# Two-layer attention and FFN kernel on one core: which units stand in front of the scores, how the projection triples are dealt over the slots, and one visit for a head group's contexts

## The reference, cut to what matters

```python
xn = _layernorm(x)
s = L0_attn(xn)          # qkv = xn @ qkv_w + qkv_b; 32 heads of D = 16; rope on q and k
                         # scores = q k^T / 4 + causal mask; softmax; ctx = probs @ v; ctx @ out_w + out_b
g = silu( (silu(xn @ W_gate.T) * (xn @ W_up.T)) @ W_down.T )     # F = 1376, kept as 11 tiles of 128
x = x + s * g
xn = _layernorm(x)
s = L1_attn(xn)          # 4 layers of a recurrence with an MLP, as a scan over 512 positions
g = silu( octonion FFN of xn with ternary weights )
x = x + s * g
```

## Time and profile before

| | |
|---|---|
| three runs | 627.14, 627.68, 629.33 us; median 627.68 |
| the profiled execution | 627.55 us, of which the span is 625.6 us |
| PE busy | 603.1 us (96%), 3368 matmuls |
| POOL, DVE, ACT busy | 388.1, 380.0, 297.6 us |
| slots 0 to 10, first and second pass | 39.5 us and 37.5 us |

### The profile page before, as it was taken

How to read it: one execution, slowest core, us unless ns; L and a number is a source line. 1 busy time by engine, 2 the same in 40 slices (tenths; PEclk the granted TensorE clock), 3 DMA queues, 4 the chain that set the end, 5 groups by cost and what they waited for, 6 DMA issues and landing times.

```text
span 625.6 us, 9856 instructions
## 1 busy us (share of the span) xinstructions
PE 603.1 (96%) x3368; PEld 418.3 (67%) x3368; DVE 380.0 (61%) x908; ACT 297.6 (48%) x460; POOL 388.1 (62%) x598
## 2 busy tenths in 40 slices
PE   6997999999999999989999999999999999999996
PEld 5875655656657888656555666688887676767664
DVE  5955868666526489667686663265986261516257
ACT  3634767555643633356665557346122344232432
POOL 6776967555334578779576544346988495731364
PEclk9998999999999999999999999999999999999999
DMA  8797684744522327667768554835410000000002
GB/s 290 242 305 220 169 237 140 222 133 110 145 67 68 102 84 205 170 187 205 208 175 231 168 144 145 312 99 187 164 73 1 0 2 1 0 1 1 0 35 101
DMA packets 60369, 83.63 MB, mean 134 GB/s; under 512 B 17936, under 2 KB 26768, under 8 KB 60320
## 3 DMA queue, kind: packets, MB, share of 16 engines
q1 hardware_dynamic: 57968, 75.02, 40.6%
q10 hardware_dynamic: 2352, 8.00, 3.4%
HBM read 65.17 MB, written 26.99 MB: 147 GB/s over the span
## 4 chain that ended last, share of the span: by engine, by line
PE 78%; ACT 4%; DVE 4%; issue 3%; POOL 1%; DMA 1%; POOLq 0%; SPq 0%; ACTq 0%; DVEq 0%
PE proj_ps L967 8%; PE proj_ps L969 6%; PE proj_ps L968 6%; PE ctx_ps L1123 6%; PE score_ps L997 4%; PE proj_ps L1171 3%; PE proj_ps L1172 3%; PE scoreT_ps L1006 3%; PE score_ps L967 3%; PE score_ps L969 2%; PE score_ps L968 2%; PE scoreT_ps L967 2%; PE scoreT_ps L968 2%; PE scoreT_ps L969 2%; DVE score_ps L1518 2%
## 5 line engine op out<-in xcount | busy, mean ns | idle before, releaser
L784 POOL TENSOR_TENSOR w_lo<-raw,w_hi 128x512 fp32r<-128x512 f32 x98 | 130.9, 1340 | 76.0 <-ACT w_hi L1336 70.5
L1518 DVE CUSTOM_DVE_ANT_0 score_ps<-score_ps,causal 128x512 f32<-128x512 f32 (+3 forms) x256 | 118.6, 519 | 66.1 <-PE score_ps L997 65.3
L1379 ACT ACTIVATE probs_T<-scoreT_ps 128x1024 f32<-128x1024 f32 x80 | 82.1, 1027 | 67.6 <-PE scoreT_ps L1006 66.1
L967 PE MATMUL proj_ps<-xn_hi,w_hi 128*128 128x512 f32 x224 | 98.9, 441 | 7.5 <-DVE gate_silu L1569 5.2
L969 PE MATMUL proj_ps<-xn_lo,w_hi 128*128 128x512 f32 x224 | 88.9, 397 | 0.0
L968 PE MATMUL proj_ps<-xn_hi,w_lo 128*128 128x512 f32 x224 | 88.9, 397 | 0.0
L967 PEld LDWEIGHTS proj_ps<-xn_hi,w_hi 128*128 128x128 f32 x224 | 42.2, 188 | 35.5 <-issue 23.1
L815 POOL TENSOR_SCALAR_AFFINE_SELECT probs_T<-probs_T 128x256 f32<-128x256 f32 x128 | 54.3, 448 | 5.6 <-ACT probs_T L1379 5.6
L942 POOL TENSOR_TENSOR hsL<-hidden_T,hsH 128x256 fp32r<-128x256 f32 x44 | 38.1, 884 | 26.6 <-ACT hsH L1458 26.1
L782 POOL TENSOR_SCALAR w_hi<-raw 128x512 fp32r<-128x512 f32 x50 | 33.9, 679 | 25.8 <-PE proj_ps L969 25.0
L969 PEld LDWEIGHTS proj_ps<-xn_lo,w_hi 128*128 128x128 f32 x224 | 42.4, 189 | 10.1
(11 more groups left out here) (314 smaller groups left out, 1351.8 us busy)
## 6 DMA issues: line engine op xcount, KB each, us to landing
raw<-w SPq DMA_DIRECT2D x98, 256.0 KB, 2.9
rows<-rows_hi SPq DMA_DIRECT2D x32, 256.0 KB, 3.4
arranged<-tern SPq DMA_DIRECT2D x96, 85.0 KB
q_st<-rows SPq DMA_DIRECT2D x32, 200.0 KB
k_st<-rows SPq DMA_DIRECT2D x32, 200.0 KB
rows<-rows_lo SPq DMA_DIRECT2D x16, 256.0 KB, 4.0
gate_w<-arranged ACTq DMA_DIRECT2D x4, 704.0 KB, 6.5
up_w<-arranged ACTq DMA_DIRECT2D x4, 704.0 KB, 7.5
```

The source lines that it names most:

```text
L784: nc.gpsimd.tensor_tensor(w_lo[n % SPLIT][:, :], raw[n % RAW][:, :], F32(w_hi[n % SPLIT][:, :]), ALU.subtract).then_inc(unit_ready, 1)
L967: nc.tensor.matmul(acc, lh, rh, start=first, stop=False)
L1379: nc.scalar.activation(probs_T[g % 2][x][:, :, :], scoreT_ps[:, :, :], ACT.Exp, scale=0.25).then_inc(probs_ready, 1)
L1518: m = nc.vector.tensor_tensor_reduce(out=block, in0=block, in1=causal[:, S - w:], scale=1.0, scalar=-3e38, op0=ALU.add, op1=ALU.max, accum ...
```

## The change

Four things are altered. (1) `Q_UNIT` and `K_UNIT`: the second quarters of q and k become units 6 and 7, in front of slot 0; the first two pairs of the FFN become units 8 to 11. DVE then does both rotations in front of its row maxima of slot 0 (`units_after(0)`), and the FFN results of slot 0 behind them; `rope_slot`, `rounded_in` put the rounding, the rest and the writes one slot earlier for these two. (2) `pv_in`: all four key tiles of a group in one visit, in slot 11 + 5g. (3) ACT's copy of the sums moves to slot 12 + 5g and the turn to slot 14 + 5g. (4) `triple_slot` reads a table, made by `deal()`: it adds up what each slot holds besides triples, gives triples by the room that is left, at most 3 in a slot as a rule, and starts no unit u before the second slot after the one in which unit u - 2 ended. Slots 16, 21, 26, 31, 36 and 41 (context visits) get no triple, slot 44 gets 4.

```diff
-Q_UNIT, K_UNIT, V_UNIT = (0, 8, 12, 18), (1, 9, 13, 19), 2
-FFN_UNIT = [6, 7, 10, 11, 14, 15, 16, 17] + list(range(20, 34))
+Q_UNIT, K_UNIT, V_UNIT = (0, 6, 12, 18), (1, 7, 13, 19), 2
+FFN_UNIT = [8, 9, 10, 11, 14, 15, 16, 17] + list(range(20, 34))
...
 def triple_slot(k):
-    room = [290 - 43 * (s < TASKS) - 33 * (s >= LAG) - 71 * (s >= 11) for s in range(SCORE_SLOTS)]
-    if k < IN_FRONT:
-        return -1
-    part = (k - IN_FRONT) * sum(room)
-    return next(s for s in range(SCORE_SLOTS) if part < (TRIPLES - IN_FRONT) * sum(room[:s + 1]))
+    return DEAL[k]
...
+def rope_slot(u):
+    return unit_slot(u) - (u == Q_UNIT[1])
+
+def rounded_in(s):
+    return [u for u in sorted(QK_OF) if u >= FILL and rope_slot(u) + 3 == s]
...
-    return [u for u in sorted(QK_OF) if u >= FILL and unit_slot(u) + 4 == s]
+    return [u for u in sorted(QK_OF) if u >= FILL and rope_slot(u) + 4 == s]
...
+PV_VISITS = ((0, 1, 2, 3),)
+PV_FIRST = LAG + 6
+
 def pv_in(s):
-    g, kt = divmod(s - 11, PARTS)
-    return (g, kt) if s >= 11 and g < GROUPS and kt <= NT else None
+    g, x = divmod(s - PV_FIRST, PARTS)
+    return (g, PV_VISITS[x]) if 0 <= g < GROUPS and x < len(PV_VISITS) else None
+
+def pv_copied_in(s):
+    g, x = divmod(s - PV_FIRST, PARTS)
+    return g if 0 <= g < GROUPS and x == len(PV_VISITS) else None
 
 def ctx_in(s):
-    return (s - 16) // PARTS if s >= 16 and (s - 16) % PARTS == 0 and (s - 16) // PARTS < GROUPS else None
+    g, x = divmod(s - PV_FIRST, PARTS)
+    return g if 0 <= g < GROUPS and x == 3 else None
+
+def deal():
+    held = [43 * (score_in(s) is not None) + 33 * (prob_in(s) is not None) + 22 * (max_in(s) is not None) + 53 * (ctx_in(s) is not None)
+            + (sum((14, 86, 64, 43, 22)[kt + 1] for kt in (-1, *pv_in(s)[1])) if pv_in(s) else 0) for s in range(SCORE_SLOTS)]
+    triple = 70
+    length = (triple * (TRIPLES - IN_FRONT) + sum(held)) / SCORE_SLOTS
+    at, room = [-1] * IN_FRONT, 0
+    for s in range(SCORE_SLOTS):
+        room += length - held[s]
+        while len(at) < TRIPLES and (room >= triple / 2 and at.count(s) < 3 or held[s] + triple * at.count(s) < 230):
+            k = len(at)
+            if k % KC == 0 and at[k - KC - 1] >= max(s - 1, 0):
+                break
+            at.append(s)
+            room -= triple
+    return at + [SCORE_SLOTS - 1] * (TRIPLES - len(at))
...
                 for u in units_after(0):
-                    if u in FFN_OF:
-                        ffn_out(b, u)
+                    if u in QK_OF:
+                        rope_times(b, u)
+                        rope_second(b, u)
```

More of the change, by code:

```diff
@@ L111, in split_in_slot @@
     return [u for u in range(FILL, U_DOWN + SPLIT) if (unit_slot(u - SPLIT) + 1 + (u >= U_DOWN) if u - SPLIT >= FILL else 0) == s]
+def rope_slot(u):
+    return unit_slot(u) - (u == Q_UNIT[1])
+def rounded_in(s):
+    return [u for u in sorted(QK_OF) if u >= FILL and rope_slot(u) + 3 == s]
 def rest_in_slot(s):
-    return [u for u in sorted(QK_OF) if u >= FILL and unit_slot(u) + 4 == s]
+    return [u for u in sorted(QK_OF) if u >= FILL and rope_slot(u) + 4 == s]
 def written_in(s):
-    return [u for u in sorted(QK_OF) if u >= FILL and unit_slot(u) + 5 == s]
+    return [u for u in sorted(QK_OF) if u >= FILL and rope_slot(u) + 5 == s]
 def read_in(s):
@@ L1113, in _ @@
                         turn(b, ("ctx", g), [ctx_sums[:, t * P:(t + 1) * P] for t in range(NT)])
-                    if pv_in(s) and pv_in(s)[1] < NT:
-                        g, kt = pv_in(s)
-                        if kt == 0:
+                    if pv_in(s):
+                        g, tiles = pv_in(s)
+                        if 0 in tiles:
                             pe.wait_ge(probs_masked, TASKS * b + PARTS * (g + 1))
@@ L1120, in _ @@
                                 pe.wait_ge(ctx_copied, GROUPS * b + g)
-                        for h in range(4):
-                            x, c = block_at(h // 2, kt)
-                            m = nc.tensor.matmul(ctx_ps[32 * h:32 * h + 32, kt * P:S], V[:, kt, (4 * g + h) * 32:(4 * g + h + 1) * 32],
-                                                 probs_T[g % 2][x][:, h % 2, c:c + S - kt * P], start=kt == 0, stop=kt == NT - 1,
-                                                 skip_group_check=True)
-                        if kt == NT - 1:
+                        for kt in tiles:
+                            for h in range(4):
+                                x, c = block_at(h // 2, kt)
+                                m = nc.tensor.matmul(ctx_ps[32 * h:32 * h + 32, kt * P:S], V[:, kt, (4 * g + h) * 32:(4 * g + h + 1) * 32],
+                                                     probs_T[g % 2][x][:, h % 2, c:c + S - kt * P], start=kt == 0, stop=kt == NT - 1,
+                                                     skip_group_check=True)
+                        if NT - 1 in tiles:
                             m.then_inc(pv_done, 1)
@@ L1379, in _ @@
                         nc.scalar.activation(probs_T[g % 2][x][:, :, :], scoreT_ps[:, :, :], ACT.Exp, scale=0.25).then_inc(probs_ready, 1)
-                    if pv_in(s) and pv_in(s)[1] == NT:
-                        g = pv_in(s)[0]
+                    if pv_copied_in(s) is not None:
+                        g = pv_copied_in(s)
                         act.wait_ge(pv_done, GROUPS * b + g + 1)
@@ L1390, in _ @@
                             rope_copy(b, u)
-                    for u in units_after(s - 2):
-                        if u in QK_OF:
-                            rope_hi(b, u)
+                    for u in rounded_in(s):
+                        rope_hi(b, u)
                     if max_in(s) is not None:
```

7 lines of the change are left out of this document (4 added, 3 removed).

## The result

The changed kernel takes 624.09 us (median of 8 runs, 621.62 to 625.91) against 627.72 of the kernel before: a ratio of 0.9936, 95% interval 0.9914 to 0.9958. The forecast was 615. Of the 12.8 us forecast, 3.6 came. The one visit, together with the new numbers of triples, gave more than forecast; the front gave nothing, because PE found a new wait and the low clock behind it; and the rotations in slots 18 to 20 cost more than forecast.

A forecast was written before the change was run, and what follows sets the result against it. PE was taken as the bound. Visits 7.8 plus front 7.8, less 2.25 taken back and 0.6 for moved rotations, gave 12.8 us off 627.55: 614.8, forecast as 615 us, range 608.5 to 621.

The forecast's parts named there:

- What bounds the kernel, and which waits the front removes: PE bounds, busy 603.1 of 625.6 us; the new front removes slots 3 and 4's waits and low clock: 7.8 us.
- What the front takes back: Slots 0 to 2: moved copies and rotations delay PE by 1.05 us a pass, plus 0.15 once: 2.25 us lost.
- Moved, not removed: Rotations of units 12, 13, 18, 19 keep their DVE and ACT work; waits in slots 10 and 19 to 22 cost 0.6 us more.
- Term 1: Context visits on PE: one visit for four takes 2.39 us, not 2.69; with fewer entries and runs, 7.8 us saved.
- DVE and ACT become the bound: Rival: groups 0 to 2 lose their 0.5 us each, slot 1 waits 1.6, slot 3 0.7: 621 us; chance 0.11.
- The front's wait only moves: Rival: slot 1 waits 2.7 us with the low clock behind, as slot 3 did; 622 us; chance 0.06.
- The constant per key tile: Rival: the visit's constant is paid for each key tile, so Term 1 falls to 2.8 us: 620 us; chance 0.11.
- the masks of POOL: Rival: contexts, now earlier in their slot, wait for POOL's masks; at 1.5 us each for twelve visits, 633 us; chance 0.04.

## Why the prediction was wrong

**What bounds the kernel, and which waits the front removes: right.** PE's busy time fell by 6.6 us, and the gate's and the hidden result's waits of slots 3 and 4 went. With POOL held back the front alone brought 5.05 us, against 5.55; but 2.6 us of wait stayed there with the old numbers of triples, and little of the forecast loss came, so the sum agrees better than its terms.

**"What the front takes back": this step failed.** It put three rotation instructions at 0.60 to 1.18 us each and took a wait of 0.7 us out of 0 to 1.6 ahead of slot 1's scores. Measured: 2.33 and 2.45 us, and the low clock behind it in both passes, some 1.5 us each. Two things were off. The bound came from the earlier trace rows, where one rotation stands half beside a split; in the changed kernel all six stand beside splits, and they took 1.17 us on average from start to start, up to 1.77 long. And the step let unit 7's rotation begin when its copies end, at 37.3; DVE was still in unit 6's, whose three took 3.3 us. The Trainium skill (SBUF — State Buffer, SBUF: two separate sides) speaks of an exclusive lock between DVE and GpSimd, also for DVE instructions with two SBUF inputs; the run with POOL held back agrees (0.69 us each). The prediction named the rule, gave 1.6 by it, and still took 0.7: even 1.6 had been worked out for three instructions, not six. Nor did the step price the low clock, which slot 3's 2.70 us had behind it in the rows. Forecast for the front 5.55 less, measured 1.3 more: 6.8 of the 8.7 us by which the profiled execution missed the 614.8.

**"Moved, not removed": too small.** The places were right (the turn in slot 19, 0.76 against 1.0; slots 20 to 22, 1.78 against 1 to 1.5), the sum was not. Slots 11 to 21 hold three groups' visits a pass; at 0.6 each, an estimate from slots 22 to 36, they should have saved 3.6 us in both passes, and they lost 0.3. So by this estimate the waits there cost 3.9 us more than before, where 0.6 was forecast; 1.7 of it is the low clock in the second pass. The walk missed that DVE stands at the division of the contexts with the rotations behind it: with the rotations ahead of it the wait of 1.78 us was 0.09.

**Term 1: right in kind, too small in size.** The visit takes 2.29 us, not 2.39, and the three groups of slots 22 to 36 save 1.6 and 1.9 us: 0.55 to 0.65 a group against 0.50. Over both passes that is about 9.3 us (3.5 there, 2.2 in the rest of the passes, 3.6 in slots 11 to 21 by the estimate above) against 7.8. But it is not the visit's alone, as the term had it: without the new numbers of triples the visits saved 0.6 us a pass in slots 22 to 36, a third of this.

**The rivals.** "DVE and ACT become the bound" came nearest: slot 1's wait was its condition, its price for it (1.8) too small, and the visits did not lose. "The front's wait only moves" is what happened in the front, at nearly its price (slot 1 waits as slot 3 did, with the low clock), but with 0.06 for it. The constant per key tile and the masks of POOL did not come, though with the better order on DVE the masks cost 0.76 us in slot 21. What came is those two together: 614.8 + 6.8 (front) + 3.3 (moved) - 1.5 (visits) = 623.4, where the profiled execution took 623.5. The terms are differences between stretches of the same two executions, so that they add up is no further proof.

**Open.** Whether the clock falls behind a wait is not a matter of its length alone. It fell behind 1.77 us in slot 21 of the second pass and not behind 1.78 in the first, nor behind 2.25 in slot 3 of the second pass before. And it fell behind far shorter ones: with the visits alone, two waits of 0.76 us in slots 20 and 21 had it behind them in both passes (PE in the first pass, and the stretch around it, granted clock 0.81).

```profile
106.79 0.42 PE L1023 MATMUL one_turn_ps<-ident_r,max_cols 128*34 128x128 f32 x4 [0.76 <-POOL max_cols L847]
107.97 0.50 PE L1037 MATMUL score_ps<-k_st,q_st 50*128 50x384 f32 x4 [0.76 <-DVE row_max L1558]
```

```profile
104.00:113.00 9.00, 7.48 (x46) 4.15 (x48) 5.55 (x17) 4.10 (x6) 7.52 (x13) 0.81 0.70 185
```

Nor is it settled by the waits of a slot: 1.42 us in slot 4 had the low clock behind it in both passes with the numbers alone, and the same wait had not in the changed kernel without the front. Which earlier idle time counts was not tried.

## What to carry to other kernels

Before work with two operands in SBUF is moved on DVE, look at what POOL does at the place it goes to: beside POOL's own such work it took 1.7 times as long here (7.04 us for six instructions against 6 x 0.69), and holding POOL back for 4.6 us was cheaper than the overlap. Price a forecast wait of PE with the low clock as a chance of its own: it cost 1.5 to 1.7 us here behind waits of 1.8 to 2.5, and no length was found below which it stayed away. When a long visit takes the place of short ones, spread the filler work anew at the same time: alone, the visit won nothing.

## What the runs showed of the hardware

- DVE's 128x512 tensor_tensor on two SBUF operands takes 0.69 us with POOL still, and up to 1.78 beside POOL's splits; POOL's tensor_tensor is stretched too, from 1.28 to 1.60. DVE's row maxima, whose scores lie in PSUM, stay at 0.68 to 0.73 in both.
- Eight matmuls whose result nobody uses (2.0 us), in the wait of 2.3 to 2.5 us of each pass, made the kernel 4.4 us faster.
- The clock fell to 1.2 GHz behind two waits of 0.76 us within two slots, and did not behind one of 2.25.
- Four key tiles of contexts in a row pay the change of form once: 2.29 us for 1280 columns a head, 0.16 over the columns.
